# First layer's routed rows written after the plan, in tile order, with static addresses

## The reference, cut to what matters

```python
# layer 0, mixture of experts: one expert a token
logits = tokens @ Wr + br                      # 2048 tokens, 8 experts
expert = argmax(softmax(logits));  max_prob = that probability
h = relu(tokens @ W1[expert] + b1[expert])     # 128 -> 256
y = h @ W2[expert] + b2[expert]                # 256 -> 128
x = x + tanh(g_ffn[0]) * max_prob * y
# layer 1: attention again, then two experts a token, gated silu, 128 -> 256 -> 128
```

## Time and profile before

| | |
|---|---|
| median of 3 runs | 452.27 us (449.35 to 452.77) |
| the profiled execution's own time | 455.05 us, span 453.3 us |
| mean granted TensorE clock | 0.855 of full speed |
| busy: PE, PE weight load | 339.5 us (75%), 249.3 us (55%) |
| busy: DVE, ACT, POOL | 253.6 us (56%), 156.5 us (35%), 149.8 us (33%) |
| moved by transfers | 70.42 MB, mean 155 GB/s |
| PE busy, tenths in 40 slices of 11.3 us | 2468979888969776466887999997577719988870 |
| granted clock, tenths | 9867699998695899569869999999787867999995 |
| transfer engines busy, tenths | 7436987940044283776440231013565366869934 |

### The profile page before, as it was taken

The page is one execution under the profiler, slowest core; times in us unless marked ns, Lnnn a source line. Parts: engine busy times, 40 slices in busy tenths (PEclk is TensorE's granted clock), DMA queues, the critical chain, the costliest instruction groups (busy, mean ns, idle before and its releaser), DMA issues. The chain is left out here.

```text
span 453.3 us, 6857 instructions
## 1 busy us (share of the span) xinstructions
PE 339.5 (75%) x2066; PEld 249.3 (55%) x2066; DVE 253.6 (56%) x846; ACT 156.5 (35%) x370; POOL 149.8 (33%) x172
## 2 busy tenths in 40 slices
PE   2468979888969776466887999997577719988870
PEld 2236545545435665465664575653277609878770
DVE  2759565666365566136747677865463604535542
ACT  2312344434322253124222455362221305444440
POOL 3211211215040340431062102274536565645560
PEclk9867699998695899569869999999787867999995
DMA  7436987940044283776440231013565366869934
GB/s 268 128 75 158 300 230 220 290 133 17 2 148 136 78 246 101 242 219 164 106 129 6 62 80 48 14 35 91 196 199 168 119 172 191 284 187 324 371 139 139
DMA packets 67908, 70.42 MB, mean 155 GB/s; under 512 B 7933, under 2 KB 50691, under 8 KB 67872
## 3 DMA queue, kind: packets, MB, share of 16 engines
q1 hardware_dynamic: 41904, 52.24, 39.6%
q10 hardware_dynamic: 22448, 11.41, 8.7%
q0 software_dynamic: 3520, 6.34, 4.3%
HBM read 40.66 MB, written 21.81 MB: 138 GB/s over the span
## 5 line engine op out<-in xcount | busy, mean ns | idle before, releaser
L963 PE MATMUL ps_s<-xT,fw 128*128 128x128 f32 x488 | 77.7, 303 | 17.0 <-DVE xT L1301 8.6
L963 PEld LDWEIGHTS ps_s<-xT,fw 128*128 128x128 f32 x488 | 69.4, 215 | 20.1 <-DVE xT L1301 10.4
L668 ACT ACTIVATE probs<-ps_s 103x512 f32<-103x512 f32 (+1 forms) x96 | 56.2, 596 | 65.4 <-PE ps_s L872 57.8
L1152 DVE TENSOR_REDUCE negm<-ps_a 128x4 f32<-128x308 f32 x128 | 55.1, 470 | 29.5 <-PE ps_a L852 23.1
L574 POOL DMA_INDIRECT routed<-pay,slot x48 | 48.0, 1001 | 57.1 <-DVE slot L1261 45.9
L592 POOL DMA_INDIRECT expert_out<-xt x46 | 45.8, 996 | 35.1 <-ACT xt L733 25.2
L852 PE MATMUL ps_a<-ks,qs 128*128 128x308 f32 x128 | 42.3, 366 | 10.4 <-DVE negm L1152 5.5
L1291 DVE SCALAR_TENSOR_TENSOR qr<-qr,ps_s 128x256 f32<-128x256 f32 x46 | 19.2, 418 | 53.9 <-ACT qr L723 32.6
L871 PE MATMUL ps_s<-qs,ks 128*103 128x512 f32 (+1 forms) x96 | 47.7, 496 | 1.9 <-issue 0.7
L548 POOL TENSOR_SCALAR ve<-mv 128x4 f32<-128x4 f32 x16 | 3.7, 230 | 121.1 <-DVE mv L1102 121.1
L872 PE MATMUL ps_s<-augT,aug 128*103 128x512 f32 (+1 forms) x96 | 40.3, 420 | 0.0
(11 more groups left out here) (156 smaller groups left out, 559.6 us busy)
## 6 DMA issues: line engine op xcount, KB each, us to landing
fw<-f_in SPq DMA_DIRECT2D x46, 384.0 KB
routed<-xt ACTq DMA_DIRECT2D x2, 5568.0 KB, 23.8
fw<-f_in SPq DMA_DIRECT2D x30, 321.0 KB
qs<-qhl SPq DMA_DIRECT2D x128, 64.0 KB, 2.0
xt<-routed SPq DMA_DIRECT2D x46, 65.0 KB
xt<-routed SPq DMA_DIRECT2D x30, 64.0 KB
routed<-xt SPq DMA_DIRECT2D x30, 64.0 KB
routed<-pad SPq DMA_DIRECT2D x18, 65.0 KB, 2.1
```

The costliest lines, as they stand in the source:

```text
L668: nc.scalar.activation(probs[0:KSIZE[j], s, :], ps_s[(NS * n + s) % SCORE_BANKS][0:KSIZE[j], :], ACT.Exp, scale=SCALE).then_inc(exp_ok, 1)
L963: last = nc.tensor.matmul(up_bank[j % 2][:, c * P:(c + 1) * P], weights_of(j)[:, c * P:(c + 1) * P], xT[j % 2][:, :], start=True, stop=True)
L1152: nc.vector.tensor_reduce(negm[:, i, g * HPG:(g + 1) * HPG], a[:, 0:GK].rearrange("p (h k) -> p h k", h=HPG), AX.X, ALU.max, negate=True). ...
```

## The change

In layer 0 the row number is no longer known when a batch's ranks are: it is now the rank plus the first row of its expert's tiles in the order of the plan, so the tiles of a part lie one behind the other in 15 blocks. So `plan(p)` comes first and `close_ranks(p)` (five new DVE instructions within it) writes the slots of both batches at once; the eight scatters of the part follow at plan + 1 to plan + 4, two a step. The rows of part 0 wait in `pay[0]` and those of part 1 in `pay[1]`, so layer 0's `normalise2` waits for no scatter. Part 0's ranks and plan come at the steps 39 and 40 (before: 40 and 42). The fills cover 15 blocks instead of 87, at the steps 1 and 2. Rows are loaded from, and returned to, fixed addresses; the register loads for them are gone, and the block half of layer 0's plan (five DVE instructions) too. Part 1's first rows are loaded from step 65 on instead of step 69. Batch 6's front in layer 1 is one step later.

```diff
-FILL_AT = [1, 14]
+FILL_AT = [1, 2]
...
+PLANNED = {"ranks": 27, "plan": 28}
...
-    {"gather": 90, "results": 99, "stats": 99, "normalise": 100, "turn": 101, "project": 102, "high": 103, "low": 103},
+    {"gather": 90, "results": 99, "stats": 99, "normalise": 101, "turn": 102, "project": 103, "high": 104, "low": 104},
...
+    if l == 0 and stage.startswith("scatter"):
+        return at_step(b // PART_NB * PART_NB + PART_NB - 1, "plan") + 1 + 2 * (b % PART_NB) + int(stage[-1]) // 2
+    if n == PART_NB - 1 and stage in PLANNED:
+        return NS * b + PLANNED[stage]
...
+        def pay_of(n):
+            return pay[0 if n >= NB else part_of(n)]
...
             def load_rows(p, t):
-                if t % SLOTS == 0:
-                    rows_from[p].update(offsets(p, 1, t, min(SLOTS, TILES[p] - t), (DUMMY + (0 if p // 2 else TILES[p] - 1)) * P * ROW[p // 2]))
+                if p // 2 and t % SLOTS == 0:
+                    rows_from[p].update(offsets(p, 1, t, min(SLOTS, TILES[p] - t), DUMMY * P * PAY))
...
             def tile_rows(p, t):
-                size = P * ROW[p // 2]
+                if p // 2 == 0:
+                    return routed[p][t * P:(t + 1) * P, :]
+                size = P * PAY
...
-                        if k == TILE_AT[p] + max(-1, t - ROWS_AHEAD):
+                        if k == TILE_AT[p] + max(-5 if p % 2 else -1, t - ROWS_AHEAD):
                             load_rows(p, t)
...
             def scatter(n, i):
-                    pool.wait_ge(slot_ok, n + 1)
+                    pool.wait_ge(slot_ok, PARTS // 2 + n - NB + 1 if l else part_of(n) + 1)
...
             def fill_rows(p):
-                act.dma_start(routed[p].rearrange("(k p) c -> p k c", p=P), bcast(zeros, 1, DUMMY + TILES[p])).then_inc(filled[p], 16)
+                act.dma_start(routed[p].rearrange("(k p) c -> p k c", p=P), bcast(zeros, 1, TILES[p])).then_inc(filled[p], 16)
...
             def normalise2(n):
-                if n >= 2:
-                    dve.wait_ge(scattered[n - 2], 16 * TPB * CHOICES[(n - 2) // NB])
-                normalise(xs(n), lambda i: pay[0][:, (n % 2) * TPB + i, 0:D], mv2, rstd2, nrm2_ok)
+                if n >= NB:
+                    m = n - NB if n < NB + 2 else n - 2
+                    dve.wait_ge(scattered[m], 16 * TPB * CHOICES[m // NB])
+                normalise(xs(n), lambda i: pay_of(n)[:, (n % 2) * TPB + i, 0:D], mv2, rstd2, nrm2_ok)
...
+            def close_ranks(p):
+                link(nc.vector.tensor_tensor(first_row[:, :], cum[:, :], tiles[:, :], ALU.subtract))
+                link(nc.vector.tensor_scalar(first_row[:, :], first_row[:, :], float(P), None, ALU.mult))
+                link(nc.vector.tensor_tensor(moved[:, :, :], chosen[:, :, :, :].rearrange("p b t e -> p (b t) e"), bcast(first_row[:, :], 1, PART_NB * TPB), ALU.mult))
+                link(nc.vector.tensor_reduce(offset[:, :], moved[:, :, :], AX.X, ALU.add))
+                at = slice(p * PART_NB * TPB, (p + 1) * PART_NB * TPB)
+                nc.vector.tensor_tensor(slot[0][:, at], offset[:, :], place[:, :, :].rearrange("p b t -> p (b t)"), ALU.add).then_inc(slot_ok, 1)
...
             def plan(p):
                 link(nc.vector.tensor_reduce(cum[:, :], cumx[:, :, :], AX.X, ALU.add))
+                if l == 0:
+                    close_ranks(p)
                 jj = cst[:, C_J:C_J + nt]
                 link(nc.vector.tensor_tensor(le[:, 0:nt, :], bcast(cum[:, :], 1, nt), bcast(jj, 2, E), ALU.is_le))
+                if l == 0:
+                    link(nc.vector.tensor_reduce(ej[:, 0:nt], le[:, 0:nt, :], AX.X, ALU.add))
+                    nc.vector.tensor_scalar(meta[p][0:1, 0, :], ej[0:1, 0:nt], float(E - 1), float(P * FW[l]), ALU.min, ALU.mult).then_inc(meta_ok, 1)
+                    return
```

More of the change, by code:

```diff
@@ L191, in sem @@
             return ctx.enter_context(nc.semaphore(name))
-        routed = [nc.dram_tensor(f"routed{p}", ((DUMMY + (1 if p // 2 else TILES[p])) * P, ROW[p // 2]), F32, kind="Internal").ap() for p in range(PARTS)]
+        routed = [nc.dram_tensor(f"routed{p}", ((DUMMY + 1 if p // 2 else TILES[p]) * P, ROW[p // 2]), F32, kind="Internal").ap() for p in range(PARTS)]
         expert_out = nc.dram_tensor("expert_out", (CHOICES[1] * TOKENS, D), F32, kind="Internal").ap()
@@ L263, in two_layers @@
         ohs = sb("ohs", [P, TPB, E], BF16)
+        chosen = sb("chosen", [P, PART_NB, TPB, E], BF16)
+        place = sb("place", [P, PART_NB, TPB])
+        first_row = sb("first_row", [P, E])
+        moved = sb("moved", [P, PART_NB * TPB, E])
+        offset = sb("offset", [P, PART_NB * TPB])
         run = [sb(f"run{p}", [P, PART_NB + 1, E], BF16) for p in range(PARTS)]
@@ L575, in scatter @@
                         out=routed[part_of(n)], out_offset=bass.IndirectOffsetOnAxis(ap=slot[c][:, t:t + 1], axis=0),
-                        in_=pay[c][:, (b % 2) * TPB + i, 0:ROW[l]], in_offset=None).then_inc(scattered[n], 16)
+                        in_=(pay[c] if l else pay_of(n))[:, (b % 2) * TPB + i, 0:ROW[l]], in_offset=None).then_inc(scattered[n], 16)
             def second_copy(n):
@@ L908, in routed_T @@
                 pe.wait_ge(nrm2_ok, n + 1)
-                transposes(lambda i: pay[0][:, (n % 2) * TPB + i, 0:D], pay_tr, nT2_ok, n + 1)
+                transposes(lambda i: pay_of(n)[:, (n % 2) * TPB + i, 0:D], pay_tr, nT2_ok, n + 1)
             def router(n):
@@ L1209, in choose @@
                 dve.sem_inc(ring_used, 1)
-                best(lg, mx[0], oh[0])
+                first = oh[0] if l else chosen[:, b % PART_NB, :, :]
+                best(lg, mx[0], first)
                 if l == 0:
                     nc.vector.tensor_tensor(shifted[:, :, :], lg[:, :, :], bcast(mx[0][:, :], 2, E), ALU.subtract).then_inc(sh_ok, 1)
-                    link(nc.vector.tensor_copy(ohs[:, :, :], oh[0][:, :, :]))
-                    src = oh[0]
+                    link(nc.vector.tensor_copy(ohs[:, :, :], first))
+                    src = ohs
                 else:
@@ L1240, in gate_and_slots @@
                 picked, row = (wt, lg2), (slotf, wm)
+                if l == 0:
+                    picked, row = (wt,), (place[:, b % PART_NB, :],)
                 dve.wait_ge(ex_ok, n + 1)
@@ L1250, in gate_and_slots @@
                 for c in range(CHOICES[l]):
-                    last = nc.vector.tensor_tensor(picked[c][:, :, :], rk[:, :, :], oh[c][:, :, :], ALU.mult)
+                    last = nc.vector.tensor_tensor(picked[c][:, :, :], rk[:, :, :], oh[c][:, :, :] if l else chosen[:, b % PART_NB, :, :], ALU.mult)
                 link(last)
@@ L1284, in plan @@
                 nc.vector.tensor_scalar(meta[p][0:1, 0, :], ej[0:1, 0:nt], float(E - 1), float(P * FW[l]), ALU.min, ALU.mult)
-                nc.vector.tensor_scalar(meta[p][0:1, 1, :], bj[0:1, 0:nt], float(DUMMY + (0 if l else nt - 1)), float(P * ROW[l]), ALU.min, ALU.mult).then_inc(meta_ok, 1)
+                nc.vector.tensor_scalar(meta[p][0:1, 1, :], bj[0:1, 0:nt], float(DUMMY), float(P * PAY), ALU.min, ALU.mult).then_inc(meta_ok, 1)
             def hidden(j):
```

9 lines of the change are left out of this document (4 added, 5 removed).

## The result

The changed kernel took 440.92 us (median of 4 runs, 438.03 to 442.48), the kernel before beside it 452.17 us (449.35 to 452.77): a ratio of 0.9729, with a 95% interval of 0.9682 to 0.9777. That is 11.3 us by the medians where 19.3 were forecast: the sign and the range held, the size was too large by 8. Run again later, beside other runs of the kernel before (median 450.95), the changed kernel took 434.60 us, a ratio of 0.9636 [0.9583, 0.9689].

What follows compares the result with a forecast made beforehand. No engine full: all follow an in-order list of steps, so each stage's last-ending wait counts. 5.9 + 5.3 + 3.6 + 4.5 = 19.3 us off 452.27 gave about 433 us, range 424 to 447.

Steps and rivals of the forecast that it cites:

- Fills: Batches 2 and 3's query spreads: smaller, earlier fills remove three PE waits (4.4 us) and restore the clock (1.5): 5.9 us.
- Rival two: At the query spreads: SP, not the fills, delays them; 13.4 us gained, 438.9 us; chance 0.05.
- Batch 1's `normalise2`: Layer 0: moved scatters shorten PE's wait by 0.9 us and the clock stays up, 4.4: together 5.3 us.
- Rival one: The waits go but the clock does not follow: 11.4 us gained, 440.9 us; chance 0.15.
- the rule of the Trainium skill: DVE `tensor_scalar` and GpSimd instructions lock each other out; if scatters too, batch 2's gain shrinks by about 1.0 us.
- Part 0: Plan, scatters, rows: bias addition no longer beside batch 2's `normalise2`, 1.6 us, and clock may stay up, 2.0: 3.6 us.
- rival three: At both plans: runs of eight scatters make engines stand, 13.2 us each; chance 0.09 for one, 0.06 for both.
- the rows come early: Between parts 0 and 1: first rows land about 180 instead of 186.9 us; 4.5 us taken, between 1 and 7.1.
- the cap: Step 77: late last return puts gathered results at 195 us, DVE's addition due at 194, capping what early rows give.

Runs made afterwards that it cites:

- e2: Changed kernel with the fills as before, 87 blocks a part, issued at steps 1 and 14: 437.65 us, ratio 0.9743.
- first pair: The profiles of the kernel before and the changed kernel from the first session: profiled executions of 455.05 and 442.48 us.
- e6: Kernel before, with POOL's bias addition of batches 1 to 3 held until the normalise2 of the batch ahead is done: 445.92 us, ratio 0.9859.
- before: The kernel before the change, as profiled in the first session: profiled execution 455.05 us, median of its runs 452.17 us.
- e5: The kernel before once more, no edit, with a second profile: 452.01 us, ratio 0.9994.
- after: The changed kernel, as profiled in the first session: profiled execution 442.48 us, median of its runs 440.92 us.
- e1: The changed kernel again, no edit, with a second profile: 434.60 us, ratio 0.9636.
- e3: Changed kernel with part 1's first rows loaded from step 69 again instead of 65: 434.19 us, ratio 0.9610.
- e7: Changed kernel with the returns of tiles 11 to 14 of parts 0 and 1 issued by ACT instead of SP: 431.16 us, ratio 0.9511.
- e9: e7 with part 1's first rows loaded from step 69 instead of 65: 437.28 us, ratio 0.9689.
- e11: e7 with POOL's bias addition of batches 1 to 3 sent behind normalise2 of the batch before: 428.66 us, ratio 0.9489.
- e4: Changed kernel with the gather of layer 1's batch 1 at step 77 instead of 73: 433.29 us, ratio 0.9631.
- e8: Changed kernel without batch 3's four scatters in part 1, its first-layer mixture missing from the output: 431.60 us, ratio 0.9545.
- e10: e9 with each of part 1's eight scatters waiting for one more finished tile of part 0: 432.39 us, ratio 0.9601.
- second pair: The profiles of the same two kernels run again without edit: e5 for the kernel before, e1 for the changed kernel.

## Why the forecast had the sign and not the size

**Fills (5.9 forecast): right for the kernel before.** Both pairs lead by 5.2 and 5.0 us at matmul 288 and by 6.7 and 6.2 behind the last of the three waits (95 us); the transfers land in 2.0 us, all three waits are gone, and the clock behind the first is 1.00. Rival two (SP delays the spread) is out. Put back into the changed kernel the fills cost less, 3.05 us by the medians (e2).

**Batch 1's `normalise2` (5.3): the wait right, the clock only in one execution.** The wait fell by 0.9 us to 1.08, the addition standing beside it as beside batch 0's (2.07 us). The clock gave 4.6 us in the first pair, where 4.4 were forecast (10.1 against 5.5 us from 401 to 440), and nothing in the second, where the kernel before had not lost it. Rival one, in which the clock doesn't follow, gave 440.9, which is what the first session measured, but not for its reason: in that pair the clock did follow. As to the rule of the Trainium skill ("SBUF — State Buffer", "Who interferes with whom"): for the addition the trace agrees (e6: 2.93 and 2.98 us fell to 1.34 once it was out of the way). For a scatter it doesn't: batch 2's four instructions took 1.34 us beside a scatter of 1.16. The 1.0 us that the rule would have taken did not go. A small price is there: the four instructions take 1.12 us with neither beside them (batch 3 here, batch 0 in e6), and the scatter beside them takes 1.16 us instead of 0.96, so some 0.2 us on either side.

**Part 0 (3.6): right.** From 440 to 572 the first pair gains 4.6 us, the second 3.1. Eight scatters with `rstd` between them and the bias addition behind them show no cost there: PE waits 0.81 us in step 47, not 3.67, and the clock behind it is 1.00, where it was 0.62 in before and 0.56 in e5.

**A term that the sum lacked: the second run of eight scatters.** This was rival three, held against the forecast at 13.2 us a run. From 650 to 742 the kernel before takes 16.0 us (e5 16.0). The eight kernels with all eight of part 1's scatters in a row take 16.3 to 19.2, mean 18.0 (after 19.2, e1 19.1, e3 19.2, e7 17.7, e9 17.0, e11 16.3; e2 and e4, which are not in the table, 19.1 and 16.3), e8 with four 15.5, e10 with eight parted 15.3. So a run of eight costs 2.6 us on the mean against e8 and e10, from 0.9 to 3.8 by the execution (e1 and e4 differ by 2.8 there, and e4's edit comes later); against the kernel before the mean loss is 2.0. The mechanism was there, its price a fifth of what layer 1's run suggested, and it varies. In the first run, of part 0, nothing of the kind is seen; there `rstd` stands between the fourth and fifth scatter, but that this is the reason wasn't tested.

**Part 1, "the rows come early" (4.5): the wait that decides was named and priced out.** The rows did come early, and the wait of 7.13 us became 0.61. The prediction had named what would catch it, the last return held back on SP's queue and step 77 behind the gather, and then priced it out: "it leaves 1 to 2 us later", and the addition at 194 against 195. Measured, the return was issued 3.1 us behind its result and the gather started 4.5 us after that. Step 77 (matmul 804) then came 11.9 us behind the first gather in after (10.9 to 11.4 in e1, e4, e7 and e8, 13.2 in e11), and 14.5 to 17.2 behind it where the rows are late (before, e3, e5, e9, e10). With early rows the gather sets step 77, with late ones the tiles do. Undoing the step changed nothing (e3). Its forecast worth is there once the return leaves early: e7 against e9, 4.7 us at step 77 and 3.6 at the end. The value taken, in the middle of 1 to 7.1, took the cap as a softener of the gain, when it was the bound that decides: from there on only what moves the gather counts.

The number of this term nearly came, and that is luck. From 742 to 804 the lead grows by 3.7 us in the first pair and by 4.0 in the second, and 3.0 and 2.8 of it are left at 915. But e3, with the rows late, gains 2.5 and 2.2 us on before and on e5 up to 804, and 4.7 and 4.3 up to 915. So it isn't the early rows that give it. One candidate is SP: in the kernel before the first rows leave 2.9 us behind the last return (182.17, 185.06), with the register loads between them, in e3 1.1 us behind it (163.40, 164.48). No run here tests that.

```profile
182.17 0.38 SPq L483 DMA_DIRECT2D routed<-xt  x1
182.72 0.35 SPq L461 DMA_DIRECT2D fw<-f_in  x1
```

**The sum.** By the table, the first pair leads by 12.3 us at 440, where the fills and batch 1's `normalise2` were to give 11.2, and gains 4.6 up to 572, where part 0 was to give 3.6. It then loses 3.2 under the second run of scatters, for which the sum had nothing, gains 3.7 up to step 77, and loses 5.0 from there to the end, where the sum had nothing either; 3.6 of these lie in the experts of after's execution alone. That leaves 12.65 of 19.3. The second pair leads by 7.2 at 440, since e5 kept the clock, gains 3.1 up to 572, loses 3.1 under the scatters, gains 4.0 up to step 77 and ends at 11.6. So what made the forecast too large is the run of scatters in both pairs, the clock in one and the end in the other. That the first session's 440.9 is the number of rival one is chance. What separates the sessions by 1% isn't a step of the change: e1's profile and after's agree up to 915, and 6.2 us of difference arise behind that, 4.0 of them in layer 1's experts, which the change leaves as they are.

**Left open.** Why PE, DVE and ACT slow down while POOL issues eight indirect transfers in a row; e8 and e10 (one profile each) show that it goes when the run is short or broken, not what it is. Why a return takes 4 to 6.5 us from its issue to the gather, on SP's queue as on ACT's. Also why the same fill lands sooner in the changed kernel (e2), and where the 4.9 us between the medians of e9 and e10 arise.

## What to carry to other kernels

When a transfer is moved ahead on an in-order queue, list what it passes and ask which of those is the last to be waited for downstream; if that one decides the next stage, the early transfer gives nothing, and issuing the overtaken one from another engine gave here what the early one promised. An experiment that undoes a step measures its worth beside the waits that are there: e3 showed nothing, e9 about 4 us. A sum can come near in a term whose mechanism is wrong; only undoing the step showed it. A gain put down to the clock should be counted only after a second profile of the kernel before shows the low level again.

## What the runs showed of the hardware that was not expected

- The granted clock after the same wait in the same place: 0.51 over 10 us behind 2.01 us of idle PE (before), and 1.00 behind 1.99 us in another execution of the same kernel (e5).
- POOL's eight indirect transfers in a row slow PE, DVE and ACT without being waited for: 61 to 81 matmuls in 14 us beside eight in a row (six executions), 85 beside four, 86 beside eight with a pause of 2.8 us in the middle, all at clock 1.00. From 650 to 742 it is 16.3 to 19.2 us with the run and 15.3 to 16.0 without (e8, e10, before, e5).
- The last 64 KB return of part 0, issued among weights of 321 KB each, let the gather go 4.5 us after its issue (169.32 to 173.80; 163.40 to 168.03 in e3), more than the 2.0 us to landing of the query transfers on the same queue. From ACT's queue it was no quicker: 5.2 us in e7 (164.70 to 169.93) and 6.6 in e9 (164.38 to 170.93).
- A POOL addition over 128x512 that overlaps DVE's four `tensor_scalar` instructions makes them take 2.07 to 2.98 us instead of 1.12; a scatter beside them makes it 1.34, and itself takes 1.16 us instead of 0.96.
